# LayerNorm statistics of the routing stage: one wide bn_aggr and a ScalarE square root in place of the VectorE Newton chain

## The chip, the cores and the metric

The kernel runs as one program on the eight cores of one Trainium2 chip. Each core does its own share of the work, with no exchange between the cores. A time is microseconds (us) of device time of the slowest core. The core shown is core 7, the slowest in the profiled execution.

Engines: PE is TensorE, DVE is VectorE, ACT is ScalarE, POOL is GpSimd, SP is SyncE (here it only issues DMAs).

## The reference

The input `x` is 2 x 8192 x 1024. The output is `x + s * silu(f)`, where `s` is a linear-attention block with an MLP and `f` is a routed mixture over 64 slots. Both start from the same normalised input:

```python
def _layernorm(x, axis=-1, eps=1e-5):
    m = jnp.mean(x, axis=axis, keepdims=True)
    v = jnp.var(x, axis=axis, keepdims=True)
    return (x - m) / jnp.sqrt(v + eps)
...
xn = _layernorm(x, axis=-1)
# routing, from xn (T = 8192 rows per batch entry, 64 slots, top 8):
h = gelu(concat([xn, slot_mean]) @ w1 + b1)
route_logits = (h @ w2 + b2) / (abs(tau) + 0.1)
topk_vals, topk_idx = top_k(route_logits, 8)
alpha = (one_hot(topk_idx, 64) * softmax(topk_vals)[..., None]).sum(-2)
slot_input = einsum('bts,btd->bsd', alpha, xn)
denom = alpha.sum(axis=1) + 1e-08
```

Then follow a GRU step and an attention over the slots (small), the linear attention and the MLP on each core's own rows, and the product.

## The kernel before

A core owns 2048 rows of `x`, but routing sums over all 8192 rows of its batch entry, so each core runs routing over all 8192. This first stage is where the change is. It goes over `N_MT` = 16 tiles of 512 rows (`mt`, each four strips `st` of 128 rows); tiles 0 to 3 are the core's own, and are kept in float32 in `XN`. After it come the slot stage (L777 and on), the linear attention (L1314 and on) and the MLP (L1759 and on), each behind barriers of all engines.

The order of the work is written out by hand, engine by engine, in lines L440 to L745. Every step counts a semaphore up (`sdv` of DVE, `spe` of PE, `sac` of ACT), and the formulas `VB`, `TB`, `AB`, `v_apply`, `t_si`, `a_exp` and so on say which count stands for which step. For a tile `mt` the engines do this:

- SP loads tile `mt` into `xld` (two tiles of room) once DVE is done with tile `mt-2`.
- DVE, `emit_head(mt)`: for each strip `ln_stats` (L231): two `bn_stats` over 512 columns each (L234, L235), a drain, one `bn_aggr` on each (L237, L238). Then `ln_combine` (L240: seven operations on 128x4 that join the halves, with eps) and `newton_rstd` (L210: 15 operations on 128x4, an integer start value, three Newton steps and a copy, a drain behind each). Then four `tensor_scalar` (L513) that write `(x - mean) * rstd`: to `XN` for own tiles, to `xnb` in bf16 for the rest. For `mt` from 4 on, the head first waits for `t_si(mt-2)`, PE's slot products of tile `mt-2`, since it will write over the `xnb` that they read.
- DVE, `emit_tail(mt-1)`, behind it: waits for ACT's logits of tile `mt-1` (`a_log`), finds the top 8 (L527), the bias of the exp (L534, L539) and the mask (L544), waits for ACT's exps (L550, L556) and writes the routing weights (L564). For own tiles it then waits for four transposes of PE and copies them to `ALPHAT` (L573).
- ACT: `emit_exp(mt-1)` (L682, L691), which waits for that DVE bias; for own tiles four copies `XN` to `xnb` (L710); four copies of PE's transposes to `xnTs` (L718); four gelus (L727); the logits to `LOG` (L736).
- PE: four groups of eight transposes of `xnb` (L632), 32 matmuls by `w1` (L646), the logits (L660, L666), and `emit_si(mt-1)`, the slot products of tile `mt-1` (L596, L598, L601).

So DVE runs head 0, head 1, tail 0, head 2, tail 1, and so on; ACT runs tile 0, then exp 0 and tile 1, then exp 1 and tile 2, and so on. `ACT_TABLE_LOAD` instructions are put in by the compiler where the next function of ACT is not in the table that is loaded. The same `ln_stats`, `ln_combine` and `newton_rstd` also serve the MLP stage, and are left as they are there.

Of the kernel before, what the change touches and what calls it, by code (L numbers as in the profile page):

```python
# [6 lines left out]
F32 = mybir.dt.float32  # L7
BF16 = mybir.dt.bfloat16
I32 = mybir.dt.int32
AF = mybir.ActivationFunctionType  # L10
# [66 lines left out]
def build_nc(dbg=False):  # L77
# [51 lines left out]
    with ExitStack() as ex:  # L129
# [40 lines left out]
        FBC = E(nc.sbuf_tensor("FBC", [128, 4], F32))  # L170
        ST = E(nc.sbuf_tensor("ST", [128, 64], F32))
        SCAL = E(nc.sbuf_tensor("SCAL", [128, 8], F32))
# [85 lines left out]
        with ExitStack() as exW:  # L258
# [6 lines left out]
            with ExitStack() as exA:  # L265
# [35 lines left out]
                with nc.Block() as blk:  # L301
# [20 lines left out]
                    @blk.gpsimd  # L322
                    def _(g):
                        cast_load(g, w1ab, w1a_d, 8, DHF, sem=swA, key='wA')
                        cast_load(g, w1bb, w1b_d, 4, DHF, sem=swA, key='wA')
# [114 lines left out]
                for m in range(N_MT):  # L440
                    VB.append(v_c); TB.append(t_c); AB.append(a_c)
                    v_c += 4 + (0 if m == 0 else
                                2 + (1 if own_f(m - 1) else 0))
                    t_c += 9 + (0 if m == 0 else
                                1 + (1 if own_f(m - 1) else 0))
                    a_c += (0 if m == 0 else 1) + (4 if own_f(m) else 0) + 9
                VB.append(v_c); TB.append(t_c); AB.append(a_c)

                v_apply = lambda m, st: dv0 + VB[m] + st + 1

                def v_tailA(m):
                    return dv0 + (VB[m + 1] + 5 if m + 1 < N_MT
                                  else VB[N_MT] + 1)

                def v_tailB(m):
                    return dv0 + (VB[m + 1] + 6 if m + 1 < N_MT
                                  else VB[N_MT] + 2)

                v_alphat = lambda m: dv0 + VB[m + 1] + 7
                t_transp = lambda m, st: pe0 + TB[m] + st + 1  # L460
# [3 lines left out]
                def t_si(m):  # L464
                    return pe0 + (TB[m + 1] + 10 if m + 1 < N_MT
                                  else TB[N_MT] + 1)

                t_alphat = lambda m: pe0 + TB[m + 1] + 11
                aoff = lambda m: (0 if m == 0 else 1) + (4 if own_f(m)
                                                         else 0)  # L470
                a_copy = lambda m, st: (ac0 + AB[m]
                                        + (0 if m == 0 else 1) + st + 1)
# [4 lines left out]
                def a_exp(m):  # L477
                    return ac0 + (AB[m + 1] + 1 if m + 1 < N_MT
                                  else AB[N_MT] + 1)
# [4 lines left out]
                with nc.Block() as blk:  # L484
# [10 lines left out]
                    def _(v):  # L495
                        def emit_head(mt):
                            own = own_f(mt)
                            v.wait_ge(sx[mt % 2], x_wait(mt))
                            if mt >= 2 and not own:
                                v.wait_ge(spe, t_si(mt - 2))  # L500
                            for st in range(4):
                                ln_stats(v, xslot(mt, st), st)
                            ln_combine(v)
                            newton_rstd(v, ST[:, 16:20], ST[:, 20:24],
                                        ST[:, 36:40], 4)
                            for st in range(4):
# [4 lines left out]
                                else:  # L511
                                    dstx = xnbs(mt, st)
                                i = v.tensor_scalar(  # L513
                                    dstx, xs, ST[:, 16 + st:17 + st],
                                    ST[:, 36 + st:37 + st],
# [160 lines left out]
                    def _(a):  # L676
# [23 lines left out]
                        for mt in range(N_MT):  # L700
                            own = own_f(mt)
                            par = mt % 2
                            if mt >= 1:
                                emit_exp(mt - 1)
# [1345 lines left out]
```

## Time and profile before

| what | us |
|---|---|
| median of 2 runs (2523.79 to 2527.59) | 2525.69 |
| the profiled execution, its own time | 2524.78 |
| its span on core 7, the slowest (first to last instruction) | 2523.2 |
| shortest span of a core (core 0) | 2498.7 |
| busy on core 7: PE / DVE / ACT / POOL | 1234.8 / 598.6 / 475.4 / 122.2 |
| the routing stage on core 7, from its first `bn_stats` to its last slot product | 96.65 to about 801.3 |

No engine is busy for even half of the span, so busy shares alone don't tell what bounds the kernel. What is to be read is who waits for whom inside a stage, and in which order. A row of the timeline gives start, duration, engine, line, operation, and in square brackets the idle time of that engine just before it with what ended it; `xN` means N instructions merged, the duration then being that of all of them.

### The profile page before, as it was taken

To read this page: it belongs to the slowest core of one execution; us is meant where nothing else is said; L and a number is where in the kernel's file an instruction comes from. 1 tells how busy PE (TensorE), PEld (TensorE's weight loads), DVE (VectorE), ACT (ScalarE), POOL (GpSimd) and SP (SyncE) were. 2 spreads that over 40 slices of the span, in tenths; PEclk is the share of its full clock that TensorE was granted. 3 is DMA by queue.
4 is the path that set the end of the run, shared out by engine and by line. 5 is a ranking of instruction groups with operands and counts; after the bars stand their busy time and mean duration, and the time that the engine had idled before them with its cause. 6 is when DMAs were issued, how large, how long until landed. Compare 5 with 4: busy or idle time off the path is not lost. (4 is left out here: it accounts for less than half of the span.)

```text
span 2523.2 us, 19587 instructions; the slowest of 8 cores (2498.7 to 2523.2 us)
## 1 busy us (share of the span) xinstructions
PE 1234.8 (49%) x6308; PEld 572.1 (23%) x6308; DVE 598.6 (24%) x1617; ACT 475.4 (19%) x712; POOL 122.2 (5%) x138
## 2 busy tenths in 40 slices
PE   0143435343443342264382663644039768598596
PEld 0021212121221110022131232222014333243242
DVE  0422342424332011032423322322040120300102
ACT  0134222232322000010020010100032141330421
POOL 1000000000000001100000000000300101101000
PEclk9966766666566655576795785867559979799798
DMA  9211111110202553524133143162971926909537
GB/s 181 56 43 58 34 67 34 35 66 34 67 0 25 107 92 50 74 56 100 59 92 71 46 98 61 59 117 66 142 118 19 118 98 66 169 1 102 98 35 99
DMA packets 341431, 183.70 MB, mean 73 GB/s; under 512 B 305171, under 2 KB 309396, under 8 KB 341332
## 3 DMA queue, kind: packets, MB, share of 16 engines
q0 software_dynamic: 182144, 72.72, 25.1%
q1 hardware_dynamic: 159188, 109.74, 15.4%
q8 instruction: 53, 0.87, 0.1%
q14 instruction: 46, 0.38, 0.0%
HBM read 204.81 MB, written 33.56 MB: 94 GB/s over the span
## 5 line engine op out<-in xcount | busy, mean ns | idle before, releaser
L632 PE MATMUL pT<-cIDb,xnb 128*128 128x128 bf16 x512 | 64.8, 307 | 379.6 <-ACTq L191 201.5
L646 PE MATMUL pM<-xnTs,w1ab 128*128 128x512 bf16 x512 | 150.6, 464 | 24.2 <-ACTq L191 24.0
L1872 DVE TENSOR_TENSOR y1t<-pTf,y1t 128x512 f32<-128x512 f32 x32 | 22.1, 691 | 516.4 <-PE pTf L1966 516.4
L632 PEld LDWEIGHTS pT<-cIDb,xnb 128*128 128x128 bf16 x512 | 49.6, 138 | 394.7 <-issue 394.7
L1935 PE MATMUL pMa<-h2T,fcwb 128*128 128x512 bf16 x512 | 127.3, 394 | 19.5 <-ACTq L191 19.5
L1935 PE MATMUL pMb<-h2T,fcwb 128*128 128x512 bf16 x512 | 122.6, 383 | 0.0
L1952 PE MATMUL pPb<-g1F,pjcb 128*128 128x512 bf16 x512 | 118.1, 391 | 7.7 <-DMA pjcb<-pjw 7.7
L1952 PE MATMUL pPa<-g1F,pjcb 128*128 128x512 bf16 x512 | 113.1, 379 | 8.9 <-ACTq L191 4.7
L1535 ACT ACT_TABLE_LOAD x4 | 5.1, 1283 | 511.1 <-PE pBig L1488 511.1
L234 DVE BATCH_NORM_STATS2 ST<-xld 128x6 f32<-128x512 f32 x64 | 44.4, 694 | 223.9 <-PE pDE L601 218.2
L1919 PE MATMUL pT0d<-cIDb,h2b 128*128 128x128 bf16 x128 | 16.3, 308 | 161.3 <-DVEq L191 100.5
L646 PEld LDWEIGHTS pM<-xnTs,w1ab 128*128 128x128 bf16 x512 | 57.5, 116 | 113.6 <-issue 79.9
L1793 POOL DMA_DIRECT2D pjcb<-pjw x32 | 53.6, 1676 | 608.3 <-PE pPa L1952 473.2
L1372 PE MATMUL pBig<-wob,aoT 128*128 128x512 bf16 x256 | 68.8, 430 | 27.1 <-DVEq L191 27.1
L718 ACT ACTIVATE xnTs<-pT 128x1024 bf16<-128x1024 bf16 x64 | 65.6, 1024 | 63.7 <-PE pT L632 61.2
L1698 DVE TENSOR_TENSOR AMK<-pBig,cMSK 128x512 bf16<-128x512 f32 x64 | 44.3, 691 | 129.7 <-PE pBig L1654 98.9
L1654 PE MATMUL pBig<-FQ2h,FK2h 64*128 64x128 bf16 x256 | 31.9, 300 | 86.2 <-DMA scr_ao<-aog 77.6
L1480 PE MATMUL pBig<-wqb,xhT 128*128 128x512 bf16 x256 | 64.7, 410 | 16.4 <-ACTq L191 16.4
L682 ACT ACT_TABLE_LOAD x16 | 20.5, 1283 | 268.7 <-DVEq L191 268.7
L1935 PEld LDWEIGHTS pMa<-h2T,fcwb 128*128 128x128 bf16 x512 | 51.0, 100 | 84.0 <-issue 27.9
L1952 PEld LDWEIGHTS pPb<-g1F,pjcb 128*128 128x128 bf16 x512 | 50.5, 100 | 70.5 <-issue 16.5
L1935 PEld LDWEIGHTS pMb<-h2T,fcwb 128*128 128x128 bf16 x512 | 50.7, 99 | 62.7 <-issue 4.0
(256 smaller groups left out, 1759.9 us busy)
## 6 DMA issues: line engine op xcount, KB each, us to landing
xld<-x8k SPq DMA_DIRECT2D x64, 512.0 KB, 7.0
pjcb<-pjw POOLq DMA_DIRECT2D x32, 1024.0 KB, 10.5
scr_qk<-tmb SPq DMA_DIRECT2D x16, 512.0 KB, 2.7
y1scr<-XN SPq DMA_DIRECT2D x4, 2048.0 KB, 7.2
fcwb<-fcw POOLq DMA_DIRECT2D x32, 256.0 KB, 20.1
y1t<-y1scr SPq DMA_DIRECT2D x4, 2048.0 KB, 11.0
xre<-x8k SPq DMA_DIRECT2D x16, 512.0 KB, 12.4
out<-xre SPq DMA_DIRECT2D x16, 512.0 KB, 3.2
```

The lines of the kernel that those rows point to most:

```text
L234: v.bn_stats(ST[:, 40:46], src1024[:, 0:512])
L632: i = t.transpose(pT0[:, cc * 128:(cc + 1) * 128], xb[:, cc * 128:(cc + 1) * 128], cIDb[:])
L646: i = t.matmul(dstp[:, 0:512], w1ab[:, cc * 512 + ch * 128: cc * 512 + (ch + 1) * 128], xnTs[:, cc * 512:(cc + 1) * 512], start=(cc == 0), ...
L718: i = a.activation(chunked(xnTs, 8, 512)[:, :, st * 128:(st + 1) * 128], chunked(pT0, 8, 128), AF.Identity)
L1372: i = t.matmul(pBig0[:, nh * 512:(nh + 1) * 512], aoT[:, cc * 128:(cc + 1) * 128], wob[:, cc * 1024 + nh * 512: cc * 1024 + (nh + 1) * 512 ...
L1480: i = t.matmul(pBig0[:, nh * 512:(nh + 1) * 512], xhT[:, cc * 512 + st * 128: cc * 512 + (st + 1) * 128], wqb[:, cc * 1024 + nh * 512: cc ...
L1654: i = t.matmul(pBig0[:, (b % 2) * 512 + gl * 128: (b % 2) * 512 + (gl + 1) * 128], FK2h[0:64, g * 128:(g + 1) * 128], FQ2h[0:64, g * 128:( ...
L1698: i = v.tensor_tensor(AMK[:, (b % 2) * 512:(b % 2 + 1) * 512], pBig0[:, (b % 2) * 512:(b % 2 + 1) * 512], cMSK[:], ALU.mult)
L1793: g.dma_start(out=dstap, in_=srcap).then_inc(spj[slot], 16)
L1872: i = v.tensor_tensor(y1v(mt).rearrange("p (s w) -> p s w", s=4)[:, :, d * 128:(d + 1) * 128], pTf[:, :].rearrange("p (s w) -> p s w", s=4 ...
L1935: i = t.matmul(dstp[:, :], fcwb[:, m * 1024 + cc * 128: m * 1024 + (cc + 1) * 128], h2T[:, cc * 512:(cc + 1) * 512], start=(cc == 0), stop ...
L1952: i = t.matmul(dstp[:, :], pjcb[:, (d % 2) * 4096 + m * 128: (d % 2) * 4096 + (m + 1) * 128], g1F[:, m * 512:(m + 1) * 512], start=(m == 0 ...
```

## The change

In the head of the routing stage the statistics are taken in another way:

- The eight `bn_stats` of a tile run one behind the other, into twelve columns of `ST` per strip, and one `bn_aggr` per strip joins both halves (four of 12 columns, where there were eight of 6 columns). `ST` grows from 64 to 96 columns.
- `ln_combine` and `newton_rstd` are gone from this stage. DVE counts `sdv` up behind the `bn_aggr`s, ACT takes `sqrt(var + eps)` of the four variances in one ACTIVATE with eps as its bias (from `SCAL[:, 7:8]`, which POOL sets once at the start), and DVE waits for it and takes the `reciprocal`.
- On ACT the square root of tile `mt` stands at the start of that tile's work, before `emit_exp(mt-1)`, so behind the logits copy of tile `mt-1`.
- The formulas of the counts are shifted by one on DVE and by one on ACT for each tile.

```diff
-        ST = E(nc.sbuf_tensor("ST", [128, 64], F32))
+        ST = E(nc.sbuf_tensor("ST", [128, 96], F32))
...
                     @blk.gpsimd
                     def _(g):
+                        g.memset(SCAL[:, 7:8], EPS)
                         cast_load(g, w1ab, w1a_d, 8, DHF, sem=swA, key='wA')
...
-                    v_c += 4 + (0 if m == 0 else
+                    v_c += 5 + (0 if m == 0 else
                                 2 + (1 if own_f(m - 1) else 0))
...
-                    a_c += (0 if m == 0 else 1) + (4 if own_f(m) else 0) + 9
+                    a_c += (1 + (0 if m == 0 else 1)
+                            + (4 if own_f(m) else 0) + 9)
...
-                v_apply = lambda m, st: dv0 + VB[m] + st + 1
+                v_aggr = lambda m: dv0 + VB[m] + 1
+                v_apply = lambda m, st: dv0 + VB[m] + st + 2
...
+                a_sqrt = lambda m: ac0 + AB[m] + 1
...
+                            v.drain()
+                            SB = (0, 40, 64, 76)
                             for st in range(4):
-                                ln_stats(v, xslot(mt, st), st)
-                            ln_combine(v)
-                            newton_rstd(v, ST[:, 16:20], ST[:, 20:24],
-                                        ST[:, 36:40], 4)
+                                v.bn_stats(ST[:, SB[st]:SB[st] + 6],
+                                           xslot(mt, st)[:, 0:512])
+                                v.bn_stats(ST[:, SB[st] + 6:SB[st] + 12],
+                                           xslot(mt, st)[:, 512:1024])
+                            v.drain()
+                            for st in range(4):
+                                i = v.bn_aggr(ST[:, 16 + 2 * st:
+                                                 18 + 2 * st],
+                                              ST[:, SB[st]:SB[st] + 12])
+                            finv(v, sdv, 'dv')
+                            v.wait_ge(sac, a_sqrt(mt))
+                            v.reciprocal(ST[:, 36:40], ST[:, 32:36])
+                            v.drain()
                             for st in range(4):
...
                                 i = v.tensor_scalar(
-                                    dstx, xs, ST[:, 16 + st:17 + st],
+                                    dstx, xs,
+                                    ST[:, 16 + 2 * st:17 + 2 * st],
                                     ST[:, 36 + st:37 + st],
                                     ALU.subtract, ALU.mult)
...
                             par = mt % 2
+                            a.wait_ge(sdv, v_aggr(mt))
+                            i = a.activation(
+                                ST[:, 32:36],
+                                ST[:, 17:25].rearrange(
+                                    "p (s two) -> p s two",
+                                    two=2)[:, :, 0:1].squeeze(2),
+                                AF.Sqrt, bias=SCAL[:, 7:8])
+                            finv(a, sac, 'ac')
                             if mt >= 1:
                                 emit_exp(mt - 1)
```

On DVE, head 0 before: the last strip's statistics, the start of `ln_combine` (L247 to L255) and of `newton_rstd` (L214 and on).

```order
L234 BN_STATS ST<-xld 128x6
L235 BN_STATS ST<-xld 128x6
L237 BN_AGGR ST<-ST 128x2
L238 BN_AGGR ST<-ST 128x2
L247 TENSOR_TENSOR ST<-ST 128x4
L248 TENSOR_TENSOR ST<-ST 128x4
L249 TENSOR_TENSOR ST<-ST 128x4
L251 TENSOR_SCALAR ST<-ST 128x4
L252 TENSOR_SCALAR ST<-ST 128x4
L253 SCALAR_TENSOR_TENSOR ST<-ST 128x4
L255 TENSOR_TENSOR ST<-ST 128x4
L214 TENSOR_SCALAR ST<-ST 128x4
```

And now on DVE, at the end of head 1 and the start of tail 0 (L528 is the old L513, L543 the old L527):

```order
L508 BN_STATS ST<-xld 128x6
L510 BN_STATS ST<-xld 128x6
L514 BN_AGGR ST<-ST 128x2 x4
L519 RECIPROCAL ST<-ST 128x4 [waits sac]
L528 TENSOR_SCALAR XN<-xld,ST 128x1024 x4
L543 MAX TKS<-LOG 128x8 [waits sac]
L543 MAX TKS<-LOG 128x8 x3
L550 TENSOR_TENSOR ST<-TKS,SCAL 128x4
```

A wait for ACT now stands inside the head; behind it on DVE are the four writes of this tile and the whole tail of the tile before.

On ACT, from tile 0 to tile 1, before:

```order
L727 ACTIVATE hFs<-pM,B1E 128x512 [waits spe] x4
L736 ACTIVATE LOG<-pLa 128x256 [waits spe]
L682 ACTIVATE E<-TKS,ST,SCAL 128x8 [waits sdv]
L682 ACTIVATE E<-TKS,ST,SCAL 128x8 x3
L691 ACTIVATE etk<-LOG,ST,SCAL 128x64 x4
L710 ACTIVATE xnb<-XN 128x1024 [waits sdv] x4
```

And now:

```order
L751 ACTIVATE hFs<-pM,B1E 128x512 [waits spe] x4
L760 ACTIVATE LOG<-pLa 128x256 [waits spe]
L720 ACTIVATE ST<-ST,SCAL 128x4 [waits sdv]
L698 ACTIVATE E<-TKS,ST,SCAL 128x8 [waits sdv]
L698 ACTIVATE E<-TKS,ST,SCAL 128x8 x3
L707 ACTIVATE etk<-LOG,ST,SCAL 128x64 x4
L734 ACTIVATE xnb<-XN 128x1024 [waits sdv] x4
```

The square root of tile 1 (L720) stands between the logits copy of tile 0 (L760, the old L736) and the exps of tile 0 (L698, the old L682).

## Rows read from the trace of the kernel before

**Rows 1.** Spans of the cores: span and mean granted TensorE clock.

```profile
core 7: 2523.2 us, clock 0.735
```

**Rows 2.** Waits from 280 to 800 us: total us, times, longest.

```profile
DVE ST L234 <- PE pDE L601: 218.2, 10, 22.9
```

**Rows 3.** Timeline of DVE, tile 8: head from 443.41, tail of tile 7.

```profile
443.41 0.69 DVE L234 BATCH_NORM_STATS2 ST<-xld 128x6 f32<-128x512 f32 x1 [22.79 <-PE pDE L601]
444.02 0.68 DVE L235 BATCH_NORM_STATS2 ST<-xld 128x6 f32<-128x512 f32 x1
444.77 0.18 DVE L237 BATCH_NORM_AGGREGATE ST<-ST 128x2 f32<-128x6 f32 x1
444.87 0.15 DVE L238 BATCH_NORM_AGGREGATE ST<-ST 128x2 f32<-128x6 f32 x1
...
454.76 3.62 DVE L513 TENSOR_SCALAR xnb<-xld,ST 128x1024 bf16<-128x1024 f32 x4
458.62 0.60 DVE L527 MAX8 TKS<-LOG 128x8 f32<-128x64 f32 x4 [0.24 <-issue]
...
459.54 0.17 DVE L539 TENSOR_SCALAR ST<-ST 128x4 f32<-128x4 f32 x1
...
463.86 0.19 DVE L550 TENSOR_REDUCE ST<-E 128x4 f32<-128x32 f32 x1 [3.29 <-ACTq L191]
464.12 0.18 DVE L556 RECIPROCAL ST<-ST 128x4 f32<-128x4 f32 x1
464.38 0.87 DVE L564 SCALAR_TENSOR_TENSOR alsc<-etk,ST,JUNK 128x64 bf16<-128x64 f32 x4
```

**Rows 4.** Timeline of ACT, from the logits of tile 7 to those of tile 8.

```profile
439.79 0.38 ACT L736 ACTIVATE LOG<-pLb 128x256 f32<-128x256 f32 x1 [1.89 <-PE pLb L666]
459.82 1.28 ACT L682 ACT_TABLE_LOAD   x1 [19.65 <-DVEq L191]
461.12 1.24 ACT L682 ACTIVATE E<-TKS,ST,SCAL 128x8 f32<-128x8 f32 x4
462.27 1.42 ACT L691 ACTIVATE etk<-LOG,ST,SCAL 128x64 f32<-128x64 f32 x4
...
484.29 0.38 ACT L736 ACTIVATE LOG<-pLa 128x256 f32<-128x256 f32 x1 [1.89 <-PE pLa L666]
```

**Rows 5.** Timeline of DVE, head 0 and the start of tail 0.

```profile
96.65 0.69 DVE L234 BATCH_NORM_STATS2 ST<-xld 128x6 f32<-128x512 f32 x1 [0.54 <-PEq L407]
...
108.40 3.62 DVE L513 TENSOR_SCALAR XN<-xld,ST 128x1024 f32<-128x1024 f32 x4
...
136.67 0.60 DVE L527 MAX8 TKS<-LOG 128x8 f32<-128x64 f32 x4 [9.15 <-ACTq L191]
```

**Rows 6.** Timeline of ACT before and in tile 0.

```profile
95.64 0.17 ACT L421 ACTIVATE JUNK<-pT 128x4 f32<-128x4 bf16 x1
...
110.61 1.06 ACT L710 ACTIVATE xnb<-XN 128x1024 bf16<-128x1024 f32 x1
...
136.11 0.38 ACT L736 ACTIVATE LOG<-pLa 128x256 f32<-128x256 f32 x1 [2.02 <-PE pLa L666]
```

**Rows 7.** Groups by line on ACT: xcount, busy us, mean ns of one.

```profile
L682 ACT ACTIVATE E<-TKS,ST,SCAL 128x8 f32<-128x8 f32 x64 | 19.9, 381 | 0.2
```

**Rows 8.** Windows from logits to logits, tiles 5 to 15, and two slot products; PEclk third from last.

```profile
439.79:484.29 44.50, 18.70 (x97) 9.39 (x96) 15.56 (x58) 12.36 (x19) 0.00 (x0) 0.62 0.14 48
...
747.25:789.90 42.65, 16.06 (x97) 8.49 (x96) 15.56 (x58) 12.36 (x19) 0.00 (x0) 0.68 0.00 1
sum 481.97, PE 194.46 PEld 99.60 DVE 171.61 ACT 136.00 POOL 0.00; mean PE 17.68 PEld 9.05 DVE 15.60 ACT 12.36 POOL 0.00
...
439.50:443.30 3.80, 3.75 (x14) 1.60 (x13) 0.00 (x0) 0.38 (x1) 0.00 (x0) 0.55 0.00 0
484.00:486.10 2.10, 2.08 (x14) 1.03 (x13) 0.00 (x0) 0.38 (x1) 0.00 (x0) 1.00 0.00 0
```

**Rows 9.** Timeline of POOL at the start of the program.

```profile
0.60 0.10 POOL L78 MEMSET const-uint8-127<- 128x1 uint8 x1
```

More of the change, by code:

```diff
@@ L445, in build_nc @@
                                 1 + (1 if own_f(m - 1) else 0))
-                    a_c += (0 if m == 0 else 1) + (4 if own_f(m) else 0) + 9
+                    a_c += (1 + (0 if m == 0 else 1)
+                            + (4 if own_f(m) else 0) + 9)
                 VB.append(v_c); TB.append(t_c); AB.append(a_c)
-                v_apply = lambda m, st: dv0 + VB[m] + st + 1
+                v_aggr = lambda m: dv0 + VB[m] + 1
+                v_apply = lambda m, st: dv0 + VB[m] + st + 2
                 def v_tailA(m):
-                    return dv0 + (VB[m + 1] + 5 if m + 1 < N_MT
+                    return dv0 + (VB[m + 1] + 6 if m + 1 < N_MT
                                   else VB[N_MT] + 1)
                 def v_tailB(m):
-                    return dv0 + (VB[m + 1] + 6 if m + 1 < N_MT
+                    return dv0 + (VB[m + 1] + 7 if m + 1 < N_MT
                                   else VB[N_MT] + 2)
-                v_alphat = lambda m: dv0 + VB[m + 1] + 7
+                v_alphat = lambda m: dv0 + VB[m + 1] + 8
                 t_transp = lambda m, st: pe0 + TB[m] + st + 1
@@ L468, in build_nc @@
                 t_alphat = lambda m: pe0 + TB[m + 1] + 11
-                aoff = lambda m: (0 if m == 0 else 1) + (4 if own_f(m)
-                                                         else 0)
-                a_copy = lambda m, st: (ac0 + AB[m]
+                aoff = lambda m: (1 + (0 if m == 0 else 1)
+                                  + (4 if own_f(m) else 0))
+                a_sqrt = lambda m: ac0 + AB[m] + 1
+                a_copy = lambda m, st: (ac0 + AB[m] + 1
                                         + (0 if m == 0 else 1) + st + 1)
@@ L477, in a_exp @@
                 def a_exp(m):
-                    return ac0 + (AB[m + 1] + 1 if m + 1 < N_MT
+                    return ac0 + (AB[m + 1] + 2 if m + 1 < N_MT
                                   else AB[N_MT] + 1)
```

## Prediction

> **What bounds the kernel now.** I read the spans of the cores first: core 7 ends last, at 2523.2 us [rows 1]. Then I looked at the routing stage alone, since the change touches nothing else. There the table of waits has one large entry on DVE: the first `bn_stats` of a head waits 218.2 us in ten tiles for PE's slot products [rows 2]. The timeline of tile 8 shows why this wait is not slack. PE's products of tile 6 end, DVE starts its head at 443.41, writes the normalised tile from 454.76, and starts the tail of tile 7 at 458.62 with 0.24 us of issue in front of it, so the logits it needs had long been there [rows 3]. ACT copied them at 439.79, then stood idle for 19.65 us until DVE's tail released its exps at 459.82 [rows 4]. The exps lead to the transposes, matmuls, gelus and logits at 484.29, and the slot products behind those open the next head. So every tile from 2 on is one closed ring, PE, DVE, ACT, PE, with hardly anything beside it. From the eleven intervals from logits to logits the sum is 481.97, 43.8 us a tile on average [rows 8]. For tiles 2 and 3 the ring is the same but for the `ALPHAT` copy before the head. What leaves the DVE head leaves the time.
>
> Two heads are different. Head 0 starts the stage, and ACT's first copy waits for it. Head 1 runs ahead: behind it DVE stands idle for 9.15 us, and tail 0 starts at 136.67, 0.18 us after the logits copy (136.11 + 0.38) [rows 5, 6]. Head 1 is hidden now.
>
> **The head in the ring, before and after.** Before, from the first `bn_stats` to the first write, it takes 454.76 - 443.41 = 11.35 us [rows 3].
>
> After, step by step from the same rows:
>
> - Eight `bn_stats` in a row. Two start 0.61 us apart, and what follows a drain starts 0.75 us after the second [rows 3]. That is 7 x 0.61 + 0.75 = 5.02 us until the first `bn_aggr`.
> - Four `bn_aggr`. Now they start 0.10 us apart and take 0.15 to 0.18 us on 6 columns [rows 3]. No row has 12 columns. They cost between nothing more (0.10 apart, end at 0.48) and twice as much (0.20 apart and 0.30 long, end at 0.90). I take 0.13 apart and 0.19 long, nearer the row, as these small operations are mostly fixed cost: 0.58. Running 5.60.
> - DVE to ACT. The bias operation L539 ends at 459.71 and the table load starts at 459.82; on the way back the last exp ends at 463.69 and DVE starts at 463.86 [rows 3, 4]. I take 0.10 and 0.17.
> - A table load. Before every exp group there is one, and the exp starts 1.30 us after it (459.82 to 461.12) [rows 4]. The square root needs one too, as exp and gelu each do now, so 16 more in all. The exps and gelus have theirs already. 1.30.
> - The square root itself on 128x4: between 0.17 us (a 128x4 ACTIVATE with no pointer operand [rows 6]) and 0.38 (128x8 with two of them [rows 7]). It has one, so I take the middle, 0.27.
> - The reciprocal, 0.26 us from its start to that of what follows [rows 3].
>
> The sum is 5.60 + 0.10 + 1.30 + 0.27 + 0.17 + 0.26 = 7.70 us. Each head in the ring gets 11.35 - 7.70 = 3.65 us shorter; by the bounds it is 3.2 to 3.85. What is late next is the same chain, since the write, the tail and the exps stand right behind. ACT is free for the square root: it idles from 440.2 until the exps, and the request comes 5.6 us into the head [rows 4]. For 14 heads (tiles 2 to 15) that is 51.1 us.
>
> At this place the Trainium skill speaks against the change. Its page "ScalarE: Activation LUTs", section "What ACT_TABLE_LOAD costs", puts a switch at about 1.28 us plus a drain of about 1.38, and advises to batch calls by table set. The trace agrees with the load but shows no such drain between load and exp or between DVE's release and the load. By the page's figure each head would give 1.38 us less.
>
> **Head 0.** From the first `bn_stats` to ACT's first copy it now takes 110.61 - 96.65 = 13.96 us [rows 5, 6], with a table load behind the first write. After, the load of the square root lies inside the 7.70 and, if copies need none of their own after it (ACT's copies that follow the exps of a tile stand in the profile without one), the copy starts 0.81 + 0.1 us behind the first write: 8.6 us. That is 5.35 less. Some 0.4 of the old 11.75 (108.40 - 96.65, against 11.35 in tile 8) looks like a chance hold-up in issue; I count half of it as staying, so 5.1. The gelus of tile 0 then need a load that they don't need now. In other tiles it hides behind the matmuls, so I cost it at nothing; uncovered, it would be 1.3.
>
> **Head 1.** Its cover is lost. The square root of tile 1 stands on ACT behind the logits copy of tile 0, and on DVE the four writes and tail 0 stand behind the wait for it. From the end of the logits copy: 0.15 for the drain and issue, 1.30, 0.27, 0.17, 0.26, then 3.62 of writes and 0.24 before the top-8 [rows 3]: 6.0 us, where it is 0.18 now. That is 5.8 us more, once.
>
> **The rest.** The `memset` on POOL stands before the weight loads that the first stage waits for; the one shown takes 0.10 us [rows 9], so at most 0.1. SP issues the loads of tile `mt+2` behind the last write of a head. These come earlier in most tiles, as do their uses, and there is a whole tile of 40 us between. The larger `ST` costs nothing. The later stages start behind barriers and simply shift.
>
> Sum: 51.1 + 5.1 - 5.8 - 0.1 = 50.3 us less. From the profiled execution's own 2524.8 (1.6 over its span) that gives 2474.5. The median of the two runs is 0.9 higher, inside their spread; I leave the number as it is and write 2474.
>
> **The clock.** A tile is not always equally long. Slot products at a granted clock of 1.00 take about 2.1 us (484.00 to 486.10), at 0.55 about 3.8 [rows 8]; the matmuls before them also run partly at half clock. So tiles come at 42.65 us (clock 0.68) and at 44.50 (0.62) [rows 8]. The change shortens the idle stretch of PE in each tile, and so moves the tiles against the changes of the clock. Nothing in the rows fixes which kind becomes more frequent. If all twelve tiles from 4 on became short it would be 12 x (43.8 - 42.65) = 14 us less, and if all became long 12 x (44.5 - 43.8) = 8 more.
>
> **The rivals.**
>
> 1. The tiles settle at the short kind: 2474 - 14 = 2460 at the limit, about 2464 if most do. For it: five of eleven are short already, and less idle time can only help the clock. Against: it would be a coincidence of lengths. Chance 0.25.
> 2. They settle at the long kind: 2474 + 8 = 2482. Likewise. Chance 0.16.
> 3. The table switch costs more than its load, by a drain or a second load in each head. One more load time of 1.30 us in 14 heads is 18 less saved: 2492. Against: nothing of it lies between load and exp, or between release and load [rows 3, 4]; it could appear only where ACT still works when the load comes, and here it idles. Chance 0.06. By the skill's page named above it would be 14 x 1.38 = 19, the same case.
> 4. Slower: the lost cover of head 1 in every tile. If heads generally ran ahead of the logits, the square root's place behind the logits copy would cost 5.8 us in 15 tiles, less 5.1 for head 0: 82 more, 2607. It decides from the point where a head's statistics end before the logits of the tile before. The wait for PE's slot products ahead of the heads (22.79 us before head 8) excludes that in tiles 4 to 15, and the `ALPHAT` wait in tiles 2 and 3. Chance 0.02.
>
> The forecast itself has 0.51.
>
> **How the numbers follow.** A measurement of this kernel can tell about 2% from no change, so "faster" begins at 2475.2 us. The forecast lies 1 us below that, with 3.2 to 3.85 us a head giving 2472 to 2481 by itself. I give it 0.58 of being beyond 2%, so 0.30. Rival 1 adds 0.25. Faster 0.55; within 2%: 0.21 of the forecast, 0.16 of rival 2 and 0.06 of rival 3, 0.43; slower 0.02. The range goes from 2462, most of the way into rival 1, to 2484, which takes in rival 2 and the dear end of the head.
>
> **What would show it.** In the profile after: 5.0 us from first `bn_stats` to first `bn_aggr`, 7.7 to the first write, 48 table loads in the stage instead of 32, tail 0 starting 6 us after the logits of tile 0, and 40.2 us from logits to logits on average. It is wrong if the write starts later than 8.2 us into the head (then the ACT round trip is dearer), if the exps don't move forward by what the head loses (then something else feeds the ring), or if the heads are right and the mean tile is off by over 0.7 us (then it is the clock).

## The result and the profile after

The changed kernel takes 2483.72 us (median of eleven runs, 2462.33 to 2574.39) beside 2524.49 for the kernel before (ten runs, 2511.01 to 2530.97). The ratio is 0.9805, with an interval of 0.9775 to 0.9835: 49 us less, between 42 and 57, and by this measurement not certain to be over 2%. The medians, here and below, hold some executions in which the cores of one die were slowed, as does the profile of "after, wait moved" (its stage is 581.1 us on that die and 580.5 on the other); the ratios leave them out. The profiled execution took 2462.35 us.

The span of the slowest core after (before: [rows 1]):

```profile
core 1: 2460.8 us, clock 0.735
```

Its waits from 266 to 746 us, as engine, tile and line, releaser, us in all, times, longest:

```profile
DVE ST L508 <- PE pDE L617: 218.5, 10, 23.1
...
ACT L720 <- DVEq L191: 88.3, 11, 9.8
```

The large wait is the one of [rows 2], unchanged: 218.5 us where it was 218.2. The part of the ring that lies outside DVE's head costs what it did. ACT's wait for DVE's tail, one stretch of 19.65 us before [rows 4], is now cut in two by the square root (L720). The head itself, DVE on core 1, one tile from its first `bn_stats` on (start, duration, line, operation, and in brackets the idle time before it and its releaser):

```profile
458.80 0.69 DVE L508 BATCH_NORM_STATS2 ST<-xld 128x6 f32<-128x512 f32 x1 [22.89 <-PE pDE L617]
459.41 0.68 DVE L510 BATCH_NORM_STATS2 ST<-xld 128x6 f32<-128x512 f32 x1
...
463.72 0.42 DVE L514 BATCH_NORM_AGGREGATE ST<-ST 128x2 f32<-128x12 f32 x4
465.97 0.18 DVE L519 RECIPROCAL ST<-ST 128x4 f32<-128x4 f32 x1 [1.82 <-ACTq L191]
466.22 3.62 DVE L528 TENSOR_SCALAR xnb<-xld,ST 128x1024 bf16<-128x1024 f32 x4
470.09 0.61 DVE L543 MAX8 TKS<-LOG 128x8 f32<-128x64 f32 x4 [0.25 <-issue]
```

And ACT in the same tile, from the logits copy to the load of the exps:

```profile
455.27 0.38 ACT L760 ACTIVATE LOG<-pLa 128x256 f32<-128x256 f32 x1 [1.89 <-PE pLa L682]
464.25 1.28 ACT L720 ACT_TABLE_LOAD   x1 [8.59 <-DVEq L191]
465.55 0.30 ACT L720 ACTIVATE ST<-ST,SCAL 128x4 f32<-128x4 f32 x1
...
471.29 1.28 ACT L698 ACT_TABLE_LOAD   x1 [5.45 <-DVEq L191]
```

From 458.80 to the first write at 466.22 the head takes 7.42 us, where it took 11.35 in [rows 3]. In it DVE stands idle for 1.82 us, the whole trip to ACT beyond the drain: load 1.28, square root 0.30, and 0.24 of hand-overs and issue. Nothing stands in ACT's way, since it had been idle for 8.59 us when the request came. The top-8 of tail follows the first write by 3.87 us (before 3.86), so what the head loses reaches the tail in full: 15.21 us from first `bn_stats` to top-8 before, 11.29 now.

Tiles 0 and 1 on DVE:

```profile
94.75 0.69 DVE L508 BATCH_NORM_STATS2 ST<-xld 128x6 f32<-128x512 f32 x1 [0.54 <-PEq L408]
...
130.66 0.18 DVE L519 RECIPROCAL ST<-ST 128x4 f32<-128x4 f32 x1 [18.83 <-ACTq L191]
...
134.78 0.61 DVE L543 MAX8 TKS<-LOG 128x8 f32<-128x64 f32 x4 [0.24 <-issue]
```

And on ACT:

```profile
100.63 1.28 ACT L720 ACT_TABLE_LOAD   x1 [6.71 <-DVEq L191]
...
103.55 1.06 ACT L734 ACTIVATE xnb<-XN 128x1024 bf16<-128x1024 f32 x1 [1.33 <-DVEq L191]
...
120.14 1.28 ACT L751 ACT_TABLE_LOAD   x1 [3.82 <-PE pM L662]
...
128.42 0.38 ACT L760 ACTIVATE LOG<-pLa 128x256 f32<-128x256 f32 x1 [1.73 <-PE pLa L682]
128.94 1.28 ACT L720 ACT_TABLE_LOAD   x1
```

Head 0 got shorter: the first copy on ACT comes 103.55 - 94.75 = 8.80 us after the first `bn_stats`, where it came 13.96 us after it [rows 5, 6]. Head 1 is the loss that the order on ACT brings. Its statistics had long been there (the reciprocal waits 18.83 us), but the square root starts only behind the logits copy of tile 0, and the top-8 of tail 0 starts 134.78 - 128.80 = 5.98 us after that copy, 0.18 before.

Table loads in the stage by line (count, busy us and mean ns, idle before them):

```profile
L720 ACT ACT_TABLE_LOAD x16 | 20.5, 1283 | 119.3 <-DVEq L191 119.2
...
L698 ACT ACT_TABLE_LOAD x16 | 20.5, 1283 | 83.3 <-DVEq L191 83.3
...
L751 ACT ACT_TABLE_LOAD x16 | 20.5, 1283 | 62.3 <-PE pM L662 62.3
```

They are 48, at 1283 ns each. A load of the third group starts only when PE's first products of `w1ab` are done, as its releaser shows, and runs beside the next ones. In tile 0, where it is new, it doesn't hold PE up: the 32 products run without a gap and take 9.42 us (from 116.48 on), where they took 9.73 before.

What ends the stage is DVE's write of `sib` behind the last slot products. After:

```profile
746.74 1.28 DVE L781 TENSOR_SCALAR sib<-pSI,ST 64x1024 bf16<-64x1024 f32 x1
```

Before:

```profile
802.09 1.28 DVE L757 TENSOR_SCALAR sib<-pSI,ST 64x1024 bf16<-64x1024 f32 x1
```

On these two cores the stage lasts 746.74 - 94.75 = 652.0 us after and 802.09 - 96.65 = 705.4 before [rows 5]. I read the same two instructions on all eight cores of every run; "stage" below is the mean of the eight. So read, it went from 704.1 to 651.2 us, 52.9 less; its cores lie between 696.6 and 706.9 before and between 647.4 and 653.2 after. What follows the stage, to which the change adds nothing, is 1714.5 us before and 1709.5 after as a mean of the cores, but from core to core and run to run it lies between 1695 and 1737 (one profile, of "after, wait moved", goes up to 1768). That spread is most of the noise of the total, and so the stage is the better measure of an edit, though each value of it comes from one execution.

### The profile page after: what moved, and what is told of

It reads as the page before. It is cut to its first block and busy times, and to the rows that moved or that the text cites. A ratio compares the mean times of both kernels' runs of the same rounds, so it can differ in the third digit from the quotient of the medians.

```text
span 2460.8 us, 18900 instructions; the slowest of 8 cores (2445.4 to 2460.8 us)
## 1 busy us (share of the span) xinstructions
PE 1248.6 (51%) x6308; PEld 576.0 (23%) x6308; DVE 536.0 (22%) x1217; ACT 500.6 (20%) x744; POOL 122.3 (5%) x139
## 5 line engine op out<-in xcount | busy, mean ns | idle before, releaser
L1559 ACT ACT_TABLE_LOAD x4 | 5.1, 1283 | 505.0 <-PE pBig L1512 505.0
L508 DVE BATCH_NORM_STATS2 ST<-xld 128x6 f32<-128x512 f32 x64 | 43.6, 681 | 220.8 <-PE pDE L617 218.5
L1722 DVE TENSOR_TENSOR AMK<-pBig,cMSK 128x512 bf16<-128x512 f32 x64 | 44.3, 692 | 126.5 <-PE pBig L1678 96.6
L1959 PEld LDWEIGHTS pMa<-h2T,fcwb 128*128 128x128 bf16 x512 | 51.1, 100 | 83.2 <-issue 26.6
L1976 PEld LDWEIGHTS pPa<-g1F,pjcb 128*128 128x128 bf16 x512 | 49.6, 99 | 72.5 <-issue 16.6
```

Of the source, the lines that this page charges most:

```text
L508: v.bn_stats(ST[:, SB[st]:SB[st] + 6], xslot(mt, st)[:, 0:512])
L1722: i = v.tensor_tensor(AMK[:, (b % 2) * 512:(b % 2 + 1) * 512], pBig0[:, (b % 2) * 512:(b % 2 + 1) * 512], cMSK[:], ALU.mult)
L1959: i = t.matmul(dstp[:, :], fcwb[:, m * 1024 + cc * 128: m * 1024 + (cc + 1) * 128], h2T[:, cc * 512:(cc + 1) * 512], start=(cc == 0), stop ...
L1976: i = t.matmul(dstp[:, :], pjcb[:, (d % 2) * 4096 + m * 128: (d % 2) * 4096 + (m + 1) * 128], g1F[:, m * 512:(m + 1) * 512], start=(m == 0 ...
```

## The experiments

All are timed against the kernel before. "Head" is the time from the first `bn_stats` to the first write, "tile" that from the logits of one tile to those of the next, both as means of tiles 5 to 15 on all cores of the profiled execution. The names e1 to e10 are those by which the expectations speak of the runs:

| Kernel | ratio to before | stage us | head us | tile us |
|---|---|---|---|---|
| before | 1 | 704.1 | 11.54 | 43.63 |
| after | 0.9805 [0.9775, 0.9835] | 651.2 | 7.47 | 40.03 |
| wide statistics alone (e1) | 0.9853 [0.9788, 0.9919] | 668.4 | 9.34 | 41.03 |
| square root alone (e2) | 0.9887 [0.9837, 0.9937] | 676.4 | 9.83 | 41.26 |
| after, square root of tile 1 early (e3) | 0.9763 [0.9701, 0.9825] | 648.3 | 7.47 | 40.2 |
| after, statistics twice (e4) | 1.0054 [1.0027, 1.0081] | 719.8 | 12.34 | 44.34 |
| after, head + 1.3 us (e8) | no interval | 667.4 | 8.78 | 40.84 |
| after, head + 2.5 us (e9) | no interval | 681.1 | 9.97 | 41.70 |
| after, wait moved (e5) | 0.95 [0.9471, 0.9529] | 580.8 | off the ring | 33.4 |
| wide statistics, wait moved (e6) | 0.9504 [0.948, 0.9529] | 577.6 | off the ring | 32.8 |
| after, filler matmuls (e7) | 0.974 [0.9709, 0.977] | 625.7 | 7.47 | 37.5 |
| wide, wait moved, fillers (e10) | 0.946 [0.9434, 0.9486] | 554.1 | off the ring | 30.7 |

**The two halves, each by itself.** The first takes only the statistics from the change and keeps the Newton steps on DVE:

```
-                            for st in range(4):
-                                ln_stats(v, xslot(mt, st), st)
-                            ln_combine(v)
-                            newton_rstd(v, ST[:, 16:20], ST[:, 20:24], ...
+                            (eight bn_stats, drain, four bn_aggr of 12 columns, drain)
+                            v.tensor_scalar(ST[:, 88:92], <the four variances>,
+                                            EPS, None, ALU.add)
+                            v.drain()
+                            newton_rstd(v, None, ST[:, 88:92], ...
```

> The kernel before with only the statistics part of the change: eight bn_stats in a row, four bn_aggr over 12 columns, one operation for eps, and the Newton chain kept on DVE. My theory (what leaves a DVE head in the ring leaves the time): from the first bn_stats to the first write 4.92 to the first bn_aggr, 0.42 + 0.07 for four, 0.24 for eps, 3.62 for Newton, 9.27 us where the kernel before has 11.35, so 2.1 less in 15 heads (0, 2 to 15), and head 1 stays hidden: about 31 us faster than before. Rival (the gain is the Newton chain's alone, drains and small aggregates cost nothing): no change from before. Rival (the clock decides): any value within +-14 of mine.

Measured: median 2496.47 us; the stage is 35.7 us shorter, for a head that is 11.54 - 9.34 = 2.20 shorter. From its timeline of DVE (core 4):

```profile
433.80 0.17 DVE L513 TENSOR_SCALAR ST<-ST 128x4 f32<-128x4 f32 x1
...
437.42 0.17 DVE L229 COPY ST<-ST 128x4 f32<-128x4 f32 x1
437.66 3.62 DVE L527 TENSOR_SCALAR xnb<-xld,ST 128x1024 bf16<-128x1024 f32 x4
```

From the start of the variance + eps (433.80) to the first write is 3.86 us of operations on 128x4 that each cost 0.24 us with their drain. This is what the trip to ACT replaces: from the end of the `bn_aggr`s it costs 466.22 - 464.14 = 2.08 us in the profile after.

The second takes only the square root and leaves statistics and `ln_combine` as they were. Its edit, against the changed kernel:

```
-                            (eight bn_stats, drain, four bn_aggr of 12 columns)
+                            for st in range(4):
+                                ln_stats(v, xslot(mt, st), st)
+                            ln_combine(v)
                             finv(v, sdv, 'dv')
                             v.wait_ge(sac, a_sqrt(mt))
...
-                                (square root of the four variances, bias EPS)
+                                (square root of ST[:, 20:24], bias 0)
```

> The changed kernel with the old statistics and combine, and only the square root on ACT with the reciprocal. My theory: a ring head is 7.66 us until the combine ends, then 0.11, 1.30, 0.30, 0.13 and 0.26: 9.76 us, 1.6 less than before in 14 heads (22), 2.9 less in head 0, 5.8 more for head 1, which is no longer hidden: about 19 us faster than before. With the wide statistics alone this adds up to the 50 of the whole change. Rival (the ACT round trip costs more than the chain it replaces): slower than before by the 5.8 and more.

Measured: median 2501.18 us, the stage 27.7 us shorter, the head 9.83. The two table loads that follow a logits copy, on ACT of the slowest core:

```profile
442.57 1.28 ACT L711 ACT_TABLE_LOAD   x1 [9.38 <-DVEq L191]
...
449.61 1.28 ACT L689 ACT_TABLE_LOAD   x1 [5.45 <-DVEq L191]
```

ACT idles for 9.38 us before the first, and it takes no longer than in the kernel with both halves. The head lengths came out as the durations said. But the gains don't add: 35.7 + 27.7 = 63.4 us where both together give 52.9. The heads do add (2.20 + 1.71 = 3.91, against 4.07), so the difference is in how a tile follows its head: each half alone brings the tile to 41.0 or 41.3 us, a drop of 2.4 to 2.6 us for 1.7 to 2.2 us of head, and the second half then brings it only to 40.0.

**The cover of head 1.** The square root of tile 1 is issued in tile 0, after the copies of `xnTs` and ahead of the gelus, and the counts follow it:

```
                            par = mt % 2
-                            (square root of tile mt)
+                            if mt != 1:
+                                emit_sqrt(mt)
...
+                            if mt == 0:
+                                emit_sqrt(1)
                             for ch in range(4):
                                 a.wait_ge(spe, t_h(mt, ch))
```

> The changed kernel with the square root of tile 1 alone moved forward on ACT, from behind the logits copy of tile 0 to before its gelus, where ACT waits 3.8 us for the matmuls. My theory: head 1 is hidden again, tail 0 starts 0.2 us after the logits of tile 0 instead of 6.0, 5.8 us less than the changed kernel, visible in the stage (first LOG to first exp table load 1.8 instead of 7.6), at the edge of what the total can show. Rival (the gelu table load, then no longer covered, takes it back): 1.3 of it given back. Rival (writes of tile 1 delay nothing): no change.

Measured: median 2472.59 us. ACT on core 4:

```profile
115.17 1.02 ACT L752 ACTIVATE xnTs<-pT 128x1024 bf16<-128x1024 bf16 x1 [1.28 <-PE pT L654]
116.34 0.30 ACT L724 ACTIVATE ST<-ST,SCAL 128x4 f32<-128x4 f32 x1 [0.16 <-issue]
...
128.29 0.38 ACT L772 ACTIVATE LOG<-pLa 128x256 f32<-128x256 f32 x1 [1.73 <-PE pLa L688]
130.05 1.28 ACT L704 ACT_TABLE_LOAD   x1 [1.38 <-DVEq L191]
```

The moved square root takes 0.30 us at 116.34 with no load ahead of it: the set of head 0's square root is still loaded after eight copies. DVE's tail 0 starts at once behind the logits again (core 4):

```profile
128.85 0.61 DVE L549 MAX8 TKS<-LOG 128x8 f32<-128x64 f32 x4 [8.21 <-ACTq L191]
```

That is 0.18 us after the copy ends, as before the change. From the start of the logits copy to the exp's load it is 1.76 us, against 7.56 (135.98 - 128.42) in the profile after: the 5.80 us of head 1 are real and have that cause. The load of the gelus takes nothing back: from the first product of `w1ab` to the logits copy it is 11.93 us here (128.29 - 116.36) and 11.94 there (128.42 - 116.48). Yet the stage is only 2.9 us shorter, since later tiles came out 0.2 us longer, with a head that had not changed. The total can't tell this kernel from the changed one: the intervals of 0.9763 and 0.9805 overlap.

**Dose: the head made longer.** In the changed kernel the eight `bn_stats` are taken twice:

```
+                            for st in range(4):
+                                v.bn_stats(ST[:, SB[st]:SB[st] + 6], ...
+                                v.bn_stats(ST[:, SB[st] + 6:SB[st] + 12], ...
+                            v.drain()
```

> The changed kernel with the eight bn_stats of each head taken twice (the same results). Each head grows by 8 x 0.593 = 4.75 us. My theory (the heads lie in the ring one for one): 15 heads, the ones of tile 0 and 2 to 15, add 4.75 each, head 1 is covered by ACT's work: 71 us slower than the changed kernel, and 4.75 more from each LOG to its exp load. Rival (part of a head is slack, hidden beside ACT or PE): clearly less, down to nothing. Rival (the clock follows the idle time): 71 +- 14, with another mix of tiles of the short and the long kind.

Measured: median 2542.86 us (eleven runs), the stage 68.6 us above that of the changed kernel, and the head 12.34 instead of 7.47. Per tile it is 4.31 us for 4.87 us of head: nearly all, but not one for one, so there is little or no slack beside the head.

Two smaller doses ask where the difference between head and tile comes from. With `range(1)` instead of `range(4)` in the added loop:

> The changed kernel with one more pair of bn_stats and a drain per head (results unchanged): head 7.42 + 1.34 = 8.76 us. Tiles 5 to 15 are 40.0 us on average in the changed kernel. Theory (the length of a tile depends on the head alone, and the clock of PE pulls it to certain lengths: 41.0 at a head of 9.29, 41.3 at 9.78): 40.9, a whole 0.9 for 1.34. Rival (head and tile one for one): 41.3.

Measured in the profiled execution (2489.28 us): head 8.78, tile 40.84, at the value that the clock theory gave.

With `range(2)`:

> The same with two more pairs: head 7.42 + 2.53 = 9.95 us. Theory: the same tile as the kernel with only the square root changed (head 9.78, tile 41.3), so 41.4 and little more, although its head is 2.5 longer than the changed kernel's. Rival (one for one from the changed kernel's 40.0): 42.5. Rival (what the head is made of matters, Newton chain or square root, and not only its length): neither.

Measured in its only execution (2509.85 us): head 9.97, tile 41.70, nearer to the theory (41.4) than to the rival (42.5). The windows from logits to logits on core 5 show how evenly its tiles come (length; busy us of PE, weight loads, DVE, ACT, POOL; granted clock, DMA share, GB/s):

```profile
475.24:516.24 41.00, 16.08 (x97) 8.46 (x96) 14.09 (x37) 13.95 (x22) 0.00 (x0) 0.67 0.14 52
516.24:557.22 40.98, 16.06 (x97) 8.46 (x96) 14.09 (x37) 13.95 (x22) 0.00 (x0) 0.67 0.14 52
557.22:598.18 40.96, 16.04 (x97) 8.47 (x96) 14.09 (x37) 13.94 (x21) 0.00 (x0) 0.67 0.14 52
```

Three tiles in a row agree within 0.04 us. In the changed kernel, with a head 2.5 us shorter, two tiles 81 us apart differ by 1.88 us, and PE is busier in the longer one for the same 97 matmuls:

```profile
455.27:496.07 40.80, 18.93 (x97) 9.47 (x96) 11.70 (x33) 13.94 (x21) 0.00 (x0) 0.62 0.14 52
...
536.28:575.20 38.92, 17.05 (x97) 8.80 (x96) 11.62 (x33) 13.88 (x22) 0.00 (x0) 0.65 0.15 55
```

The difference, 18.93 - 17.05 = 1.88 us, is the whole difference of the tiles: matmuls of the ring that ran at a lower granted clock. The same holds between the kernels: the first tile with the longer head has PE busy for 18.93 - 16.08 = 2.85 us less than the 40.80 us tile of the changed kernel, and is only 0.20 us longer for 2.55 us more of head. In order of head length (7.47, 8.78, 9.34, 9.83, 9.97, 11.54, 12.34) the mean tiles are 40.03, 40.84, 41.03, 41.26, 41.70, 43.63, 44.34. The tile grows slowly from 8.78 to 9.83 (0.42 us for 1.05), steeply between 9.97 and 11.54 (1.93 us for 1.57). On such a curve the two halves don't add.

**The wait that put the head on the ring.** The head waits for the slot products of tile `mt-2` because its writes go over `xnb`. Its statistics write only `ST`. So the wait moves down, in front of the writes:

```
                             v.wait_ge(sx[mt % 2], x_wait(mt))
-                            if mt >= 2 and not own:
-                                v.wait_ge(spe, t_si(mt - 2))
...
                             v.drain()
+                            if mt >= 2 and not own:
+                                v.wait_ge(spe, t_si(mt - 2))
                             for st in range(4):
                                 xs = xslot(mt, st)
```

On the changed kernel:

> The changed kernel with the wait for PE's slot products (t_si) moved from the start of the head to just before the four writes, which are all that it guards. My theory (the heads of tiles 4 to 15 lie in the ring only because of this wait): statistics and square root are done while PE still works, and the first write comes about 0.2 to 0.7 us after the slot products (the square root is still behind the logits copy on ACT: 0.14 + 1.30 + 0.30 + 0.13 + 0.26 after it) instead of 7.4: about 7.1 us x 12 tiles = 85 us less than the changed kernel in the routing stage, about 33 us a tile. Rival (the statistics would be late anyway, since DVE or the x loads are): nothing or little. Rival (the clock takes back part): 85 - 14 to 85 + 14.

Measured: median 2411.74 us (lowest 2395.49), the stage 70.4 us below that of the changed kernel, just below the 71 to 99 that were expected. From the timeline of core 4, all engines:

```profile
440.98 0.38 ACT L760 ACTIVATE LOG<-pLa 128x256 f32<-128x256 f32 x1 [1.97 <-PE pLa L682]
...
442.79 0.30 ACT L720 ACTIVATE ST<-ST,SCAL 128x4 f32<-128x4 f32 x1
442.87 0.17 PE L617 MATMUL pDE<-cCOL,alsc 128*64 128x1 bf16 x1
443.21 0.18 DVE L517 RECIPROCAL ST<-ST 128x4 f32<-128x4 f32 x1 [16.51 <-ACTq L191]
443.54 3.62 DVE L528 TENSOR_SCALAR xnb<-xld,ST 128x1024 bf16<-128x1024 f32 x4
```

The statistics are now taken while PE still works, and the reciprocal has waited 16.51 us for a square root that stands behind the logits copy in ACT's order. That ends at 443.09, and the slot products (last at 442.87 + 0.17) at 443.04: the square root is as late as they are. This is the condition of rival 4 of the prediction, heads that run ahead of the logits, come true; its price of 5.8 us a tile is not paid, since the writes have to wait for the slot products anyway. So the same edit on the kernel with wide statistics and Newton steps, where nothing of the head waits for ACT:

> The kernel before with the wide statistics, the Newton chain kept on DVE, and the same wait moved. My theory: once the head is off the ring it doesn't matter how rstd is computed, so in tiles 4 to 15 it is as fast as the changed kernel with the late wait, or 0 to 0.6 us a tile faster (no square root behind the logits copy); head 1 is hidden (5.8 less), heads 0, 2 and 3 are 3.1, 1.8 and 1.8 longer. Within 8 us of e5, about 140 less than the kernel before in the stage. Rival (the cheaper chain still matters through DVE's load): slower than e5 by 1.8 us x 12 = 22.

Measured: median 2399.05 us; the stage 577.6 against 580.8, and 126.5 us below that of the kernel before, where about 140 were expected. Core 3:

```profile
427.99 0.17 DVE L229 COPY ST<-ST 128x4 f32<-128x4 f32 x1 [0.42 <-issue]
...
437.42 0.38 ACT L750 ACTIVATE LOG<-pLa 128x256 f32<-128x256 f32 x1 [1.97 <-PE pLa L680]
...
439.72 3.62 DVE L527 TENSOR_SCALAR xnb<-xld,ST 128x1024 bf16<-128x1024 f32 x4 [11.56 <-PE pDE L615]
```

The last Newton operation ends 11.56 us before PE releases the writes. The slower way to `rstd` now costs nothing, and the faster one buys nothing: the two kernels differ by 3 us in the stage and not at all in the ratio (0.95 and 0.9504). The 3 us are a balance. In tiles 5 to 15 the kernel with the Newton steps is 0.56 us a tile faster (32.80 for 33.36), 6.2 us in all, the price of the square root's place on ACT with whatever the clock adds, and 3.0 us up to the logits of tile 1; in tiles 2 to 4, whose heads are still on the ring, it is 5.8 us slower. So what the square root saves in the ring (17.2 us of the stage, 668.4 to 651.2, beside the wide statistics) is saved only because of where this wait stands.

**The clock by itself.** PE gets matmuls whose result nobody reads (`w1ab` by `w1ab` into `pM0`, overwritten by the next real product), 30 behind the slot products, 28 behind the first transposes of a tile and 4 behind each of the next three:

```
+                        def emit_fill(n):
+                            for f in range(n):
+                                t.matmul(pM0[:, 0:512], <128 columns of w1ab>,
+                                         <512 columns of w1ab>, start=True, stop=True)
```

> The changed kernel with filler matmuls on PE in the places where it waits in each tile (30 of 128x512 behind the slot products, 28 behind the first group of transposes, 4 behind each other group, into pM0, from w1; results unused). It prices the clock. My theory: with the granted clock at 1.00 through the whole tile, the 32 matmuls take 6.9 us instead of 9.0 to 9.6, the slot products 2.0 instead of up to 3.7, and three exposed groups of transposes 0.5 instead of 1.0 each: 3.5 to 5 us a tile, 50 to 70 us less in the stage, and all tiles of one length. Rival (the fillers are in the way, or the clock isn't granted for them): the stage no shorter, or longer by up to 4 x 0.43 us a group.

Measured: median 2455.63 us; the stage is 25.5 us below that of the changed kernel, about half of what was expected or less. Its windows on core 7 show one reason (columns as above): the later products of `w1ab` and the logits of a tile, and behind them the slot products:

```profile
430.40:440.70 10.30, 8.66 (x53) 4.10 (x54) 0.00 (x0) 4.03 (x5) 0.00 (x0) 1.00 0.00 1
440.66:443.95 3.29, 3.29 (x14) 1.44 (x13) 0.00 (x0) 0.38 (x1) 0.00 (x0) 0.57 0.02 5
```

The products run at 1.00, but in the slot products the clock falls to its lower level all the same, though PE had been busy for 8.66 of the 10.30 us before. They take 3.29 us, nearer to the 3.80 than to the 2.10 of [rows 8]; on this core seven of the sixteen groups take 3.3 to 3.6 us and the other nine 2.01. Why the clock falls there no run shows. The other reason is that the groups of four stand partly in the way. From the timeline:

```profile
424.42 1.91 PE L632 MATMUL pM<-w1ab 128*128 128x512 bf16 x4
424.72 1.02 ACT L754 ACTIVATE xnTs<-pT 128x1024 bf16<-128x1024 bf16 x1 [1.07 <-PE pT L657]
...
426.12 1.06 PE L657 MATMUL pT<-cIDb,xnb 128*128 128x128 bf16 x8
```

Here the transposes (L657) stand directly behind a group that holds PE for 1.91 us, with no idle time between, though ACT's copy that they wait for had ended at 425.74 (424.72 + 1.02): they are late by up to 0.4 us.

The Trainium skill describes this gate on its page "TensorE: Matmul & The Clock Gate", section "HAM oscillation — how this bites in real kernels", as a cost of loops in which TensorE idles between bursts; the filler bears it out with 25.5 us. The same fillers without the 30 behind the slot products, on the kernel with wide statistics and the moved wait:

> The wide statistics with Newton on DVE and the late wait (e6), with filler matmuls of e7 only where PE waits for the exps: 28 behind the first group of transposes, 4 behind each other group. If the clock is granted for them, the 32 matmuls after them go at 6.9 us instead of 9 to 10, and a tile is 2 to 2.5 us shorter than e6's 32.8: 25 to 35 less in the stage, about 2370 in all, the fastest of all. Rival (the groups of 4 are in the way at half clock, as in part of e7's tiles, where they ended after the next group could have started): 10 less or nothing.

Measured: median 2386.78 us (2382.74 to 2391.7), the fastest of all, 0.946 of the kernel before; the stage is 23.5 us below that without the fillers, just short of the 25 expected at the least. The stretch from 262 to 670 us without the fillers (core 3):

```profile
262.00:670.00 408.00, 204.60 (x1163) 103.75 (x1164) 171.79 (x593) 152.22 (x237) 0.00 (x0) 0.68 0.14 52
```

With them (core 7):

```profile
262.00:670.00 408.00, 305.36 (x1656) 141.85 (x1656) 172.52 (x594) 152.24 (x237) 6.21 (x10) 0.83 0.19 56
```

The granted clock rises from 0.68 to 0.83. The matmuls of `w1ab` in that stretch, by line, without the fillers:

```profile
L660 PE MATMUL pM<-xnTs,w1ab 128*128 128x512 bf16 x384 | 112.4, 460 | 20.0 <-ACTq L191 19.9
```

And with them:

```profile
L671 PE MATMUL pM<-xnTs,w1ab 128*128 128x512 bf16 x384 | 94.2, 402 | 9.7 <-ACTq L191 9.1
```

Each costs 402 instead of 460 ns, and the stage falls from 577.6 to 554.1 us.

## Why the prediction was right, and where it was right by luck

It said 2474 us, 2462 to 2484, 50.3 us less; measured were 49 (42 to 57), which is 2475 by the ratio. By its own steps:

- **What bounds it.** Right. The head was on a closed ring: the wait ahead of it is unchanged, the tail follows as it did, and a longer head (statistics twice) costs nearly its whole length again.
- **The head after, 7.70 us.** Measured 7.42 in the tile shown. The statistics take 4.92 (463.72 - 458.80) instead of 5.02, since their pitch is 0.593 us and not 0.61; the four `bn_aggr` end after 0.42 instead of 0.58, so twelve columns cost about what six do; to ACT 0.11 instead of 0.10; load 1.30; the square root 0.30 and back 0.12, together 0.42, for 0.27 + 0.17; the reciprocal 0.25 instead of 0.26.
- **The head before, 11.35 us.** This is the term that was mis-sized. Tile 8 was read as if all were like it, but the mean of the heads is 11.54: of the eleven in tiles 5 to 15 seven carry a hold-up in issue, five inside the Newton steps and two in the statistics, the same seven on every core. One of them, on DVE before:

```profile
364.92 0.16 DVE L227 TENSOR_TENSOR ST<-ST 128x4 f32<-128x4 f32 x1 [0.37 <-issue]
```

The prediction had seen one in head 0, called it chance and didn't look for more. It isn't chance. Counting all of DVE's records in a trace, with drains and semaphore records, the hold-ups come 128 records apart (59, 188, 443, 572, 700, 955 and on, before; the places between fall into waits and show nothing). The changed kernel has fewer records in a tile, and only two of its heads in tiles 5 to 15 meet one (7.65 and 7.71 as means of the cores), so its mean head is 7.47, near its undisturbed length. So a head lost 11.54 - 7.47 = 4.07 us and not 3.65; 14 of them are 57 us, not 51.1.

- **Head 0, 5.1 less.** 13.96 - 8.80 = 5.16: right. Here the hold-up stayed whole (head 0 takes 7.85 us as a mean of the cores, 7.42 undisturbed), where half was counted.
- **Head 1, 5.8 more.** 5.98 - 0.18 = 5.80: right, and the run with the early square root takes exactly this back and names its cause.
- **48 loads.** Right. ACT's copies need none of their own after a square root, and the gelu's new one in tile 0 holds nothing up.
- **The clock.** The prediction left it at zero and gave the extremes to rivals 1 and 2. Its two kinds of tile were too simple: of the eleven before, on core 7, five take 44.5 to 44.6 us, three 42.7 to 43.0 and three lie between (so five of eleven were not short); after, tiles range from 38.3 to 41.6. The clock took 0.47 us of each tile back (tile 43.63 to 40.03, 3.60 for 4.07). The sum by the heads is 57.0 + 5.2 - 5.8 = 56.4 against 52.9 in the stage, so about 3.5 us were given back over the stage. The two misses, about 6 us too little for the heads and nothing for the clock, cancel in part, and the promised tile of 40.2 (measured 40.03) hit in part for that reason: the luck of the forecast.
- **Rival 3**, a dearer switch, is out. From the request to the square root it is load and hand-over, nothing else. Even at 128.94, where the load comes 0.14 us behind a logits copy that had just run, there is no drain like the one that the Trainium skill adds to each load on its page "ScalarE: Activation LUTs", section "What ACT_TABLE_LOAD costs"; here the measurement decides.
- **Rival 4**, lost cover in every tile, was rightly excluded for this kernel. The moved wait brings its condition about: with heads ahead of the logits, the square root's place behind the copy does become the limit, but at 0.56 us a tile and not 5.8.

What stays open: why tiles of nearly one length follow each other for heads between 9.3 and 10 (40.6 us at 9.34, 41.0 at 9.83 and 9.97). That the granted clock of the matmuls in the ring makes tiles differ is shown (equal counts, other busy time); which event starts each change of the clock isn't. Nor was the wait moved in the kernel before with nothing else changed.

## What to carry to other kernels

A stretch that stands on a ring is worth its full length, and its length can be added up from single instructions to a few per cent; but take the mean over all rounds of the loop, not one round. Before making such a stretch cheaper, ask what the wait ahead of it protects: here only the last four instructions needed it, and moving it brought more (70 us of the stage beyond the change, 91 beyond the wide statistics with the Newton steps kept) than the cheaper arithmetic (53). And where work goes to another engine's queue, ask what stands ahead of it there: the round trip took 2.08 us with that engine idle; in head 1, with the square root behind the logits copy, the reciprocal waited 18.83 us and the tail behind it came 5.8 us later.

## What the runs showed of the hardware that was not expected

- In a ring with PE in it, the length of a round follows an edit in steps: for heads of 8.8 to 9.8 us the mean tile is 40.8 to 41.3, between 9.97 and 11.54 it grows by 1.93 us. Gains of two edits then don't add (35.7 and 27.7 alone, 52.9 together).
- Matmuls whose result nobody reads made the stage 25.5 us shorter in one kernel and 23.5 in another, there with a granted clock of 0.83 instead of 0.68 from 262 to 670 us.
- A square root behind copies that followed another square root took no table load; the square root, exp and gelu each took one of 1283 ns when they took turns.
- Four `bn_aggr` of 12 columns ended after 0.42 us, where 0.48 was the lowest bound from those of 6 columns.
- In every trace here, all eight cores, each DVE operation that started more than 0.33 us late with nothing to wait for stands near the 60th record of a stretch of 128 (59 to 62, counted over all of DVE's records from the start). Such hold-ups, of 0.37 us in the row above and 0.42 in the kernel with wide statistics and the moved wait, cost time only where DVE isn't waiting anyway; they added 0.2 us to the mean head before (11.54 for 11.35) and 0.05 after (7.47 for 7.42). What they come from no run shows.
